# First units moved beside the scan, weights and modulations brought in another way, and the gate folded into tanh

## The reference, cut to what matters

```python
mod = (silu(c) @ wmod).reshape(B, 6, 1, D)          # sa, ca, ga, sb, cb, gb
ga, gb = (2 * (g >= 0) - 1) * max(abs(g), 0.25)     # each of the two
h = layernorm(x) * (1 + ca) + sa
omega = clip(softplus(h @ W_omega.T + b_omega), 1e-4, 100)
zeta  = sigmoid(h @ W_zeta.T + b_zeta)
F     = h @ W_B.T + b_B
# scan over t: S = 1 / (1 + DT^2 omega^2), d = 1 - zeta
z, y = d * (S*z - DT*omega^2*S*y) + F_z, d * (DT*S*z + S*y) + F_y
x = x + ga * (states @ C.T + h @ D_mat.T)
h = layernorm(x) * (1 + cb) + sb
xr, xk = mu * h + (1 - mu) * h_shifted_by_one_row   # mu_r, mu_k
x = x + gb * sigmoid(xr @ W_r.T) * (relu(xk @ W_k.T)**2 @ W_v.T)
```

## Time and profile before

| what | value |
|---|---|
| median of 3 runs | 1007.74 us (1007.02 to 1007.92) |
| the profiled execution | 1007.41 us, of which the span is 1004.8 us |
| TensorE busy | 945.0 us, 94% of the span |
| VectorE, ScalarE, GpSimd busy | 777.4, 766.8, 120.8 us |
| chain that ended last | PE 76%, ACT 10%, DVE 8% |
| granted TensorE clock | 0.986 over the span |

### The profile page before, as it was taken

How to read it: one execution, slowest core, us unless ns; L and a number is a source line. 1 busy time by engine, 2 the same in 40 slices (tenths; PEclk the granted TensorE clock), 3 DMA queues, 4 the chain that set the end, 5 groups by cost and what they waited for, 6 DMA issues and landing times.

```text
span 1004.8 us, 14776 instructions
## 1 busy us (share of the span) xinstructions
PE 945.0 (94%) x4992; PEld 784.2 (78%) x4992; DVE 777.4 (77%) x2137; ACT 766.8 (76%) x1599; POOL 120.8 (12%) x123
## 2 busy tenths in 40 slices
PE   4746999999999999999999999999999999999997
PEld 1325887888888888888888887888888888887886
DVE  0586979787878978796887978797897878797653
ACT  6768887889878787987878788887878798745541
POOL 1250011110201011010101011020101002000000
PEclk9879899999999999999999999999999999999999
DMA  7650112021211302121120302112120211111001
GB/s 246 230 188 0 65 42 75 10 84 43 73 65 43 95 17 68 43 84 44 43 95 29 104 7 84 42 53 74 43 95 6 97 35 42 43 43 43 22 22 42
DMA packets 35259, 64.77 MB, mean 64 GB/s; under 512 B 3688, under 2 KB 4328, under 8 KB 35184
## 3 DMA queue, kind: packets, MB, share of 16 engines
q1 hardware_dynamic: 35184, 63.84, 18.9%
HBM read 47.02 MB, written 16.81 MB: 64 GB/s over the span
## 4 chain that ended last, share of the span: by engine, by line
PE 76%; ACT 10%; DVE 8%; issue 2%; DMA 2%; POOL 1%; SPq 1%; DVEq 0%; ACTq 0%
PE ps_kr L302 32%; PE ps_cd L302 18%; PE ps_tv L302 13%; PE ps_pt L302 8%; PE ps_tv L344 2%; PE ps_pt L310 2%; DVE mix_full L812 2%; ACT square_out L497 1%; ACT mix_full L596 1%; DVE tmp L1013 1%; ACT rt L633 1%; ACT mix_r_hi L607 1%; ACT L633 1%; ACT h_full L525 1%; DMA mix_full<-in_w_b 1%
## 5 line engine op out<-in xcount | busy, mean ns | idle before, releaser
L812 DVE SCALAR_TENSOR_TENSOR mix_full<-ps_tv,cur_m,mix_full 128x256 f32<-128x256 f32 x256 | 121.4, 478 | 60.4 <-ACT mix_full L596 60.4
L1200 POOL TENSOR_SCALAR var<-sq 128x2 f32<-128x2 f32 (+1 forms) x48 | 29.7, 618 | 810.1 <-ACT square_out L497 810.1
L596 ACT ACTIVATE mix_full<-ps_tv,cur_m 128x255 f32<-128x255 f32 x256 | 119.9, 574 | 0.2 <-PE ps_tv L344 0.2
L615 ACT ACTIVATE kk<-ps_kr 128x512 f32<-128x512 f32 x64 | 36.5, 589 | 108.8 <-PE ps_kr L302 108.8
L302 PE MATMUL ps_kr<-mix_k_hi,wk_hi 128*128 128x256 f32 x512 | 82.4, 283 | 3.0 <-ACT rt L633 2.6
L514 ACT ACTIVATE x_in<-x_in,norm_bias,rstd 128x512 f32<-128x512 f32 x64 | 47.0, 805 | 46.8 <-POOL norm_bias L1207 46.8
L302 PE MATMUL ps_kr<-mix_k_hi,wk_lo 128*128 128x256 f32 x512 | 81.2, 280 | 0.0
L302 PE MATMUL ps_kr<-mix_k_lo,wk_hi 128*128 128x256 f32 x512 | 81.1, 280 | 0.0
L302 PEld LDWEIGHTS ps_kr<-mix_k_hi,wk_hi 128*128 128x128 f32 x512 | 70.8, 189 | 10.2 <-issue 8.5
L302 PE MATMUL ps_tv<-wv_hi,kk_hi 128*128 128x512 f32 x256 | 71.1, 399 | 5.6 <-issue 5.6
L302 PE MATMUL ps_kr<-wr_hi,mix_r_hi 128*128 128x512 f32 x256 | 71.4, 400 | 0.8 <-ACT kk L615 0.8
(11 more groups left out here) (172 smaller groups left out, 2292.9 us busy)
## 6 DMA issues: line engine op xcount, KB each, us to landing
x_in<-in_x SPq DMA_DIRECT2D x16, 1024.0 KB, 5.2
x<-in_x SPq DMA_DIRECT2D x32, 512.0 KB, 3.7
out<-x SPq DMA_DIRECT2D x32, 512.0 KB, 2.7
x<-in_wmod SPq DMA_DIRECT2D x4, 1024.0 KB, 6.4
mix_full<-in_wmod SPq DMA_DIRECT2D x2, 1024.0 KB, 7.4
x<-in_wd SPq DMA_DIRECT2D x1, 1024.0 KB, 5.0
x<-in_wr SPq DMA_DIRECT2D x1, 1024.0 KB, 7.3
x<-in_wv SPq DMA_DIRECT2D x1, 1024.0 KB, 5.5
```

What stands on the lines that cost most here:

```text
L596: mm = act.activation(mix[n][:, k, 1:UNIT], ps_tv[:, j, c * UNIT:(c + 1) * UNIT - 1], ACT.Identity, bias=cur_m[:, SHIFT + k:SHIFT + k + 1] ...
L615: act.activation(kk[:, i, :], ps_kr[:, i, :], ACT.Relu).then_inc(s_relu, 1)
L812: dve.scalar_tensor_tensor(mix[n][:, k, :], ps_tv[:, j, c * UNIT:(c + 1) * UNIT], cur_m[:, alpha + k:alpha + k + 1], mix[n][:, k, :], ALU. ...
L1200: pool.tensor_scalar(var[:, :], sq[:, :], 1.0 / D, EPS, ALU.mult, ALU.add).then_inc(s_var, 1)
```

## The change

Six things are changed together.

- Staging: weights land in tensors laid on bytes that are used only later (`stage_mix` over the mixing's high and low parts, `stage_kk` over those of k, `stage_out` over xn2 and rt), and each piece has a semaphore of its own. SyncE issues x in two halves around sa, and gb before ga.
- Modulations: sa, ca, cb and sb are formed as columns, 16 matmuls of 4 columns each (two passes, so 32 instructions), with no copy and no transposes back. ga and gb stay rows (`gate_row`).
- The first chunk: its mean and variance by bn_stats and bn_aggr on VectorE, two of four tiles normalised and two of four blocks read by VectorE, all four blocks transposed at once (`transposed_at_once`), the projections' passes in another order with the low part of h last (`first_projections`), and the reads for f done by VectorE.
- `weight_low` moves from GpSimd to VectorE.
- The first two units are written out by hand on every engine, beside the scan of chunk 1; the loop starts at unit 2.
- `gated_out` is gone: `gated_tanh` forms (tanh + 1) times gate before v, `read_out` multiplies v by it, `add_out` adds. In odd units ScalarE does tanh before the last two blocks of h.

Staging, and the order in which SyncE issues:

```diff
+        with nc.sbuf_tensor("stage_mix", [P, 2, KC, D], F32) as stage_mix:
+            pass
...
+        STAGE = {"sa": x2_a, "ca": x2_b, "proj": kk[:, :, :].rearrange("p a (c t) -> p (a c) t", c=2),
+                 "wd": stage_out, "wc": xs, "ga": x2_a, "gb": mix_place, "cb": stage_mix[:, 1], "sb": mix_place,
+                 "wk": stage_mix[:, 0], "wr": x2_b, "wv": stage_kk}
...
+            x0_half(0)
+            mod_in("sa")
+            x0_half(1)
+            for small, name in ((ident[:, :], "ident"), (scan_bias[:, :], "scan_bias"), (mu[:, :, :], "mu")):
+                sp.dma_start(small, d[name]).then_inc(s_const, 16)
+            mod_in("ca")
+            for name, at, w in (("w_omega", 0, M), ("w_zeta", M, M), ("w_b", 2 * M, 2 * M)):
+                sp.dma_start(STAGE["proj"][:, :, at:at + w], weight_piece(name)).then_inc(s_in["proj"], 16)
+            weight_in("wd")
+            sp.dma_start(xs[:, :], d["wc"]).then_inc(s_in["wc"], 16)
+            mod_in("gb")
+            sp.wait_ge(s_mod["sa"], 1)
+            mod_in("ga")
+            sp.wait_ge(s_t1, KC)
+            sp.dma_start(x_in[:, :, :], x_rows[1]).then_inc(s_xin, 16)
+            weight_in("wk")
+            mod_in("cb")
+            sp.wait_ge(s_mod["gb"], 1)
+            mod_in("sb")
+            sp.wait_ge(s_mod["ga"], 1)
+            for u in range(2):
+                sp.dma_start(x2[:, u], x_units[u]).then_inc(s_x2in[u], 16)
+            sp.wait_ge(s_mod["ca"], 1)
+            weight_in("wr")
+            sp.wait_ge(s_row, 2)
+            for g in range(2):
+                sp.dma_start(rows[g], kk[0:B, g, :]).then_inc(s_rows, 16)
+            sp.wait_ge(s_rows, 32)
+            for g in range(2):
+                sp.dma_start(gate_cols[:, 0, g, :], rows_spread[g]).then_inc(s_gate_in, 16)
+            weight_in("wv")
```

TensorE, with the new functions and its start:

```diff
+            def columns(what, bank):
+                pe.wait_ge(s_in[what], 16)
+                w = STAGE[what]
+                for m in range(KC):
+                    for k in range(KC):
+                        mm = pe.matmul(bank[:, m * B:(m + 1) * B], w[:, k, m * P:(m + 1) * P], silu_c[:, k, :],
+                                       start=(k == 0), stop=(k == KC - 1))
+                mm.then_inc(s_mod[what], 1)
...
+            def transposed_at_once(q, banks):
+                for k in range(KC):
+                    for i in range(TPC):
+                        mm = pe.transpose(banks[k // 2][:, k % 2, i * P:(i + 1) * P],
+                                          x_in[:, i, k * P:(k + 1) * P], ident[:, :])
+                    mm.then_inc(s_t1, 1)
...
+            def first_projections(q):
+                pe.wait_ge(s_h_hi, q * KC + KC)
+                for m in range(2):
+                    product(ps_pt[:, m, :],
+                            [[proj[w][:, k, m * P:(m + 1) * P] for k in range(KC)] for w in range(2)],
+                            [[h[q][w][:, k, :] for k in range(KC)] for w in range(2)],
+                            last=(s_h_lo, q * KC + KC), passes=((0, 0), (1, 0), (0, 1))).then_inc(s_p, 1)
...
-            modulation("sa")
-            modulation("ca")
+            columns("sa", ps_tv[:, 0, :])
+            columns("ca", ps_tv[:, 1, :])
             pe.wait_ge(s_const, 48)
-            pe.wait_ge(s_xn1, TPC)
-            t1_blocks(0, (0, 1))
-            row_to_columns("sa", 0)
-            row_to_columns("ca", 1)
-            rest_transposed_in(0)
-            pe.wait_ge(s_cut, CUTS.index("proj") + 1)
-            projections(0)
-            modulation("ga")
-            modulation("sb")
-            modulation("gb")
-            modulation("cb")
-            row_to_columns("sb", 2)
-            row_to_columns("cb", 3)
+            pe.wait_ge(s_xn1, 1)
+            pe.wait_ge(s_xn1_rest, 1)
+            transposed_at_once(0, (ps_pt, ps_cd))
+            pe.wait_ge(s_weight_lo["proj"], 1)
+            first_projections(0)
+            pe.wait_ge(s_tab_h, 2)
+            gate_row("gb", ps_tv[0:B, 1, :])
+            gate_row("ga", ps_tv[0:B, 0, :])
+            pe.wait_ge(s_weight_lo["wd"], 1)
+            h_part(0, ps_cd)
             pe.wait_ge(s_pev, 1)
-            pe.wait_ge(s_xn1, 2 * TPC)
-            t1_blocks(1, (0, 1))
-            rest_transposed_in(1)
-            pe.wait_ge(s_cut, CUTS.index("wd") + 1)
-            pe.wait_ge(s_row, len(MODS))
-            h_part(0, ps_cd)
-            projections(1)
+            pe.wait_ge(s_f0, 1)
+            pe.wait_ge(s_xn1, 2)
+            pe.wait_ge(s_row, 2)
+            transposed_at_once(1, (ps_pt, ps_tv))
+            h_part(1, ps_kr)
+            first_projections(1)
+            columns("cb", ps_tv[:, 1, :])
+            pe.wait_ge(s_weight_lo["wc"], 1)
+            pe.wait_ge(s_xs_first_hi, 1)
+            pe.wait_ge(s_xs_first_lo, 1)
+            states_part(0, ps_cd)
             pe.wait_ge(s_xs_hi, 1)
             pe.wait_ge(s_xs_lo, 1)
-            states_part(0, ps_cd)
-            h_part(1, ps_kr)
             states_part(1, ps_kr)
-            pe.wait_ge(s_tab_m, 1)
+            columns("sb", ps_tv[:, 0, :])
+            pe.wait_ge(s_gated, TPU)
+            h_part(2, ps_cd, (0,))
+            pe.wait_ge(s_tab_m, 2)
             t2_blocks(0)
-            pe.wait_ge(s_pev, 2)
-            pe.wait_ge(s_xn1, 3 * TPC)
-            t1_blocks(2, (0, 1))
-            rest_transposed_in(2)
+            h_part(2, ps_cd, (1,))
             def k_product(u):
...
+            k_product(0)
+            transposed_mixes_in(1)
+            r_product(0)
+            t1_first_half(2)
+            v_product(0)
+            rest_transposed_in(2)
+            k_product(1)
+            projections(2)
+            r_product(1)
+            v_product(1)
+            pe.wait_ge(s_xs_hi, 2)
+            pe.wait_ge(s_xs_lo, 2)
+            states_part(2, ps_cd)
+            t1_first_half(3)
+            pe.wait_ge(s_gated, 3 * TPU)
+            h_part(3, ps_cd)
+            pe.wait_ge(s_rv, 3 * TPU)
+            t2_blocks(2)
+            states_part(3, ps_cd)
+            rest_transposed_in(3)
+            for u in range(2, NUNIT):
```

ScalarE, its start from the weight wk on, and the odd units of the loop:

```diff
             weight_high("wk")
-            sums1(2)
-            states_out(0)
-            squares1(2)
+            weight_high("wr")
+            states_out_first()
             projections_out(1)
             softplus_parts(1)
+            statistics2(0)
+            sums1(2)
             squared_angle(1)
-            statistics2(0)
-            normalise1(2)
-            act.wait_ge(s_cut, len(CUTS))
+            statistics2(1)
             shifted(0)
             mix_high(0, 0)
+            mix_high(0, 1)
+            weight_high("wv")
+            squares1(2)
+            relu(0)
+            shifted(1)
+            relu_squared(0)
+            normalise1(2)
             h_blocks(2, (0, 1))
-            mix_high(0, 1)
-            act.wait_ge(s_xn2, TPU)
-            statistics2(1)
+            mix_high(1, 0)
+            tanh(0)
             h_high(2, (0, 1))
             h_blocks(2, (2, 3))
             h_high(2, (2, 3))
-            for u in range(NUNIT):
+            mix_high(1, 1)
+            relu(1)
+            relu_squared(1)
+            projections_out(2)
+            softplus_parts(2)
+            tanh(1)
+            sums1(3)
+            squares1(3)
+            states_out(1)
+            squared_angle(2)
+            normalise1(3)
...
                     if next_mix:
                         mix_high(u + 1, 1)
+                    tanh(u)
                     if next_t1:
                         h_blocks(q + 3, (2, 3))
                         h_high(q + 3, (2, 3))
-                    tanh(u)
```

VectorE with the gate and its start, and at the end GpSimd's part that goes:

```diff
+            def gated_tanh(u):
                 if u % UPB == 0:
                     dve.wait_ge(s_gate_b, u // UPB * 16 + 16)
                 for i in range(TPU):
+                    dve.wait_ge(s_rt, u * TPU + TPU + i + 1)
+                    dve.scalar_tensor_tensor(rt[:, i, :], rt[:, i, :], 1.0, gate_b[:, :], ALU.add, ALU.mult)\
+                       .then_inc(s_rvg, 1)
+                    yield
...
+            def read_out(u):
+                for i in range(TPU):
+                    dve.wait_ge(s_v, u * TPU + i + 1)
+                    dve.wait_ge(s_rvg, u * TPU + i + 1)
+                    dve.tensor_tensor(rt[:, i, :], ps_tv[:, i, :], rt[:, i, :], ALU.mult).then_inc(s_rv, 1)
+                    yield
...
-                    dve.tensor_tensor(rt[:, i, :], rt[:, i, :], gate_b[:, :], ALU.mult).then_inc(s_rvg, 1)
-                    yield
-                for i in range(TPU):
-                    dve.wait_ge(s_rvg, u * TPU + i + 1)
...
+            weight_low("proj")
             run(h_low(0, range(KC)))
+            weight_low("wd")
+            weight_low("wc")
+            dve.wait_ge(s_y_bias, 1)
+            dve.wait_ge(s_p, 2)
+            for n in range(2):
+                to, cols = slice(n * M, n * M + M), slice(n * HALF, (n + 1) * HALF)
```

(43 more changed lines are left out.)

410 lines of the change are left out of this document (228 added, 182 removed).

## The result

The changed kernel takes 1021.8 us (1016.3 to 1023.0), the kernel before 1007.8: 1.2% slower, ratio 1.0123 with a 95% interval of 1.0101 to 1.0146. The forecast was 992, the range 981 to 1003. The profiled execution took 1023.0 us, its span 1021.2.

A forecast was written before the change was run, and what follows sets the result against it. TensorE was taken to bound the loop, leaving the start, some waits and the end to win: 12.5 - 2 + 4 + 1.2 = 15.7 us off 1007.4 gives 991.7, 992 on the median; range 981 to 1003.

The forecast's parts named there:

- Projections of chunk 0: Start to chunk 0's projections: begin at 23.2 us instead of 27.15, a lead of 4.0, bounds 0.8 to 7.
- Scan of chunk 0: First scan: tree starts at 36.2 us, held VectorE instructions give back 9.8, gate wait 1.9; ends at 57.6 instead of 72.3.
- To the first k product: From ScalarE's read of chunk 1's projections to unit 0's k: 23.3 us as before, k at 83.4, lead 19.4.
- The pair: First two units beside scan 1: 53.4 work, 13.3 waits, 1.7 lower clock, 68.4 us; k of unit 2 at 151.8.
- Scan 2's lag: After k of unit 2, the scan of chunk 2 is behind and TensorE waits for states: minus 2, between 0 and 8.
- The loop: From unit 2 on: TensorE bound, about 28 us a unit; gated tanh and earlier tanh gain 4 us, between 0 and 6.
- The slower rival: Even units of the loop: k_low ahead of the scan's last steps delays the scan in 14 pairs, 1019 us; chance 0.05.
- Blocking turned round: Start: VectorE's long subtractions hold GpSimd's statistics, 3.4 us at two waits, 999 us; chance 0.10.
- The pair costs more: Hand-written pair: VectorE's queue behind table loads makes scan 2 8 us late, one more 3 us wait, 1001; chance 0.15.
- The long instructions aren't GpSimd's doing: First scan: VectorE's long instructions have another cause and stay, 9.8 us back, 1002; chance 0.05.
- More is kept: Start and pair: full clock in the columns (3), fewer waits in the pair, no lag of scan 2, 984 us; chance 0.13.
- The end: Behind the last v: two fewer VectorE instructions take 1.2 us off the path.

The follow-up runs named there:

- e8: Changed kernel with gated_tanh behind the residual and four scan steps beside add_out, plus nine useless matmuls on TensorE ahead of columns sa and ca: 992.5 us.
- e9: e7 with the low parts of wk and wr formed by GpSimd again instead of VectorE: 995.1 us.
- e6: Kernel before with 128 unused bytes of each partition ahead of square_out1, no instruction changed: 1006.3 us, ratio 0.9974.
- e1: Kernel before with only the loop's share of the change (gated_tanh, read_out, add_out, tanh's place on ScalarE), old start: 1027.0 us, ratio 1.0175.
- e5: Changed kernel with the loop's share undone (old read_out, gated_out and tanh's place), new start, pair and memory places kept: 1008.6 us, ratio 1.0002.
- e2: Changed kernel with gated_tanh of even units behind the residual on VectorE, nothing else: 996.8 us, ratio 0.9886.
- e7: Changed kernel with gated_tanh behind the residual, four scan steps beside add_out, and in odd units relu and shifted ahead of normalise1 on ScalarE: 984.2 us.
- e11: Kernel before with the edits of e6 and e7 (128 unused bytes; relu and shifted ahead of normalise1 in odd units), old start and gated_out: 981.6 us.
- e15: e7 with matmuls of no use filling four waits of TensorE in the hand-written pair of units: 981.1 us, ratio 0.9734.
- e10: e7 with 64 more unused bytes of each partition ahead of square_out1: 996.4 us, ratio 0.9879.

## Why the prediction was wrong

**Projections of chunk 0: wrong, the lead outside its bounds of 0.8 to 7.** The columns took 13.8 us (10.9 taken, 14.1 the upper bound); the transposes behind them 1.95 for eight (1.04 taken). "I take half at each, 10.9, since TensorE comes out of idleness" was the failed step here: e8 shows that the columns themselves run the clock down. With 2.0 of waiting for the low part of proj behind VectorE's two reads, the lead of 4.0 was 0.1.

**Scan of chunk 0: right.** The tree started at 41.1 (36.2 forecast, the 3.9 above and 1.0 more). From there to the state it took 22.0 us, forecast 21.4, with the gate's wait at 3.1 for 1.9. The 9.8 us of held instructions were real: before, the three end within 0.7 us behind a GpSimd subtraction (those end at 57.2, 65.7 and 70.8 us), and e9 brings two such holds back (4.0 us each) and pays 10.9 in the end.

**To the first k product: right.** From ScalarE's read to k 23.3 us, as forecast. k at 89.0 instead of 83.4 is the start's miss alone, 5.6.

**The pair: the waits right, the clock too small.** Forecast 3.1, 4.8, 1.4 and 4.0, 13.3 in all; measured 2.6, 4.4, 1.1 (for h's low part, not for the transposes) and 4.2, 12.3. The pair took 72.2 us, not 68.4. Work at the new pitch is about 52, so some 8 us are the lower clock and not 1.7. That puts k of unit 2 at 161.2, past the 160 that the prediction gave as its own limit.

**Scan 2's lag: right, but not all.** The wait for its states was 2.2, forecast 2. Yet this pair took 66.7 us against 56.9 before: two waits for unit 3's and 4's normalising, 0.4 for h's low part, the slow clock at its start, and the wait ahead of v.

**The loop: this sank it.** The sum was 12.5 - 2 + 4 + 1.2 = 15.7 us gained. Measured on the same terms it is 3.1 at k of unit 2, -20.7 from there to the last v, and 1.2 at the end: 16.4 lost. "So the loop is TensorE's, about 28 us a unit that no other order shortens", and the gated tanh "lets k_low of odd units come 1.2 us earlier": +4. For this and scan 2's lag the forecast was +2, and the loop came to -20.7 (833.1 to 853.8). I had read the small waits of the earlier trace rows as slack. They say only that TensorE is seldom late. A line from the residual through ScalarE, GpSimd, ScalarE and VectorE to v of the odd unit was as long as TensorE's work beside it: 0.4 to 0.9 us longer in every second pair, 0.3 to 0.5 shorter in the others. The row that shows it is the wait itself, ahead of that v. Of the gated tanh I counted what it takes from behind v in odd units, and not that in even units its 1.29 us stand ahead of the residual, the head of this line. The slower rival was about the same queue, but about k_low and the scan's state.

**What went unseen in favour:** the tiles behind square_out1 lie 128 bytes further on, and the matmuls are 2 to 4% faster, by product: rest 823.5 to 812.2 in e6. In the changed kernel the slow groups behind the longer waits ate part of it (818.0). Without it the change would have cost more; e1, which lacks it, took 1027.0 although its start is the old one.

**The rivals.** "Blocking turned round" added one hold, where it cost nothing, beside the subtraction of wv on VectorE; ScalarE came to chunk 2's normalising later than this:

```profile
93.56 2.93 POOL L1413 TENSOR_TENSOR rstd<-var,minus_half 128x4 f32<-128x4 f32 x1
```

In the loop, GpSimd's instruction of 3.27 or 1.41 us stood in the line in both kernels alike; the rival did not have it, since it looked at the start alone. "The pair costs more" was true in kind. "The long instructions aren't GpSimd's doing" fell with e9. "More is kept" had the full clock in the columns, which e8 refutes. No case had the loop's line.

**The end: right.** From the last group of v to the end of the span 7.4 us before and 6.2 after.

In all: 128 bytes -0.26% (e6), new start and pair in the old loop +0.28% (e5 against e6), the fold as written +1.2% (changed against e5). The last is made of two parts: the place of gated_tanh in even units costs 25.0 us (e2), and the rest of the fold gains 11.8 (e2 against e5). Once the line is out of the way, the whole change is worth +2.6 us (e7 against e11): the start's lead of 15.5 us at k of unit 0 goes in the pair (70.2 against 58.6 us) and in the next pair (62.6 against 55.9), 11.6 and 6.7. e15 shows the clock as a part of the first, the waits are the larger part; what order would avoid them stays open.

## What to carry to other kernels

An engine that is busy 99% of the time and hardly waits isn't proof that it alone is the bound: take one of its small, regular waits, follow it back to where the engine itself released the line, and compare the length of that line with the work beside it. If they are equal, every instruction put into the line is paid in each round, here in twelve pairs, and in four of them with a clock loss on top. Read the durations in the line too: an instruction far longer than its like elsewhere may itself be held. When work is taken off one place of an in-order queue, look at what it now stands ahead of. And an engine's long wait in mid-line is the place to move other work into (e7: one call moved, 10 us).

## What the runs showed of the hardware

- The pitch of fp32r matmuls, the time between two groups' starts, changed with where the tiles lie (e6, e10). The places are bytes of a partition, worked out from the order and sizes of the tiles. h at 0 and mix and kk at 192 (modulo 256, the weights at 128): 0.93 us for four of 128x512. With h at 128, mix and kk at 64: 0.91. With h at 192, mix and kk at 128: 0.93 for the products of h with wd, 0.91 for those of r and v, and 0.48 for four of 128x256 in k, where the two others have 0.47 and 0.454. Three places were tried, and all tiles behind the spare bytes moved together; that gives no rule, but a spread of up to 6% for nothing but an address.
- Matmuls with 4 columns don't keep TensorE's clock up: 64 of them took 13.8 us from idleness and 10.9 behind 8 us of full matmuls, and what followed ran at half pace in both.
- Behind waits of 2.5 to 4.4 us TensorE often ran its first groups at the lower level, but not always: of the changed kernel's twelve waits ahead of v (1.5 to 2.6 us) four were followed by a granted clock of 0.50, eight by 1.00. The page TensorE: Matmul & The Clock Gate of the Trainium skill, section Loop structure matters more than you think, says that a long wait between matmuls lets TensorE fall back to its lower clock; e15 agrees, with 0.45 for 0.86 us a group once the wait was filled.
- GpSimd's rstd on 128x4 took 1.01 us beside an idle VectorE and 1.40 or 3.27 in the loop, the same in every second pair, before and after.
